# A gated recurrence over 512 steps on one core: input gates placed in PSUM a pair of steps ahead, 512-column projections, and operands that arrive laid out

## The reference, cut to what matters

```python
Xz, Xr, Xh = (einsum('btc,hc->tbh', X, Wx) + bx for each gate)   # all steps at once
def step(H, xs):                                                  # 512 times, one after the other
    Z = sigmoid(xz + H @ Whz.T + bhz)
    R = sigmoid(xr + H @ Whr.T + bhr)
    H_tilda = tanh(xh + R * H @ Whh.T + bhh)
    H_new = Z * H + (1.0 - Z) * H_tilda
    Y = H_new @ Whq.T + bhq
out = x + transpose(Ys)
```

## Time and profile before

| | us |
|---|---|
| median of 3 runs (2405.9 to 2407.41) | 2407.05 |
| the profiled execution's own time | 2406.99 |
| its span, first to last instruction | 2405.2 |
| TensorE busy | 2346.3 (98%) |
| VectorE busy | 1732.1 (72%) |
| ScalarE busy | 1036.9 (43%) |

### The profile page before, as it was taken

One profiled execution on the slowest core, in us unless ns is written; L12 is line 12 of the kernel. 1 busy time (PEld: TensorE's weight loads), 2 busy tenths in 40 slices (PEclk: granted clock), 3 DMA queues, 4 the chain that ended last, 5 costly groups with the idle time before them and its releaser, 6 DMA issues.

```text
span 2405.2 us, 125877 instructions
## 1 busy us (share of the span) xinstructions
PE 2346.3 (98%) x54656; PEld 1969.8 (82%) x54656; DVE 1732.1 (72%) x10587; ACT 1036.9 (43%) x5144; POOL 0.8 (0%) x7
## 2 busy tenths in 40 slices
PE   7999999999999999999999999999999999999997
PEld 6888888888888888888888888888888888888875
DVE  5777777777777777777777777777777777777776
ACT  4444444444444444444444444444444444444443
POOL 0000000000000000000000000000000000000000
PEclk9999999999999999999999999999999999999999
DMA  5010110110100101101101001010011010110000
GB/s 163 12 30 21 30 30 12 30 29 21 30 16 25 30 21 30 28 14 29 29 21 30 16 25 30 21 30 25 16 30 27 23 30 14 28 30 21 21 14 18
DMA packets 60685, 66.06 MB, mean 27 GB/s; under 512 B 7201, under 2 KB 40033, under 8 KB 60129
## 3 DMA queue, kind: packets, MB, share of 16 engines
q1 hardware_dynamic: 60128, 58.00, 8.8%
HBM read 41.20 MB, written 16.78 MB: 24 GB/s over the span
## 4 chain that ended last, share of the span: by engine, by line
PE 80%; DVE 18%; issue 2%; DMA 0%; SPq 0%; ACT 0%; DVEq 0%
PE pre L335 45%; PE x_bank L306 26%; DVE pre_t L525 10%; PE y_bank L318 8%; DVE pre L532 6%; DVE reset_state L539 2%; DVE w_split L476 0%; DMA x_in<-in_x 0%; PE pre L289 0%; SPq L210 0%; PE y_bank L289 0%; DVE x_turned L489 0%; DVE fresh L546 0%; DVE kept L590 0%; DVE state L554 0%
## 5 line engine op out<-in xcount | busy, mean ns | idle before, releaser
L335 PE MATMUL pre<-w_gate,state 128*16 128x128 f32 x32768 | 995.5, 273 | 17.1 <-DVE state L554 16.5
L335 PEld LDWEIGHTS pre<-w_gate,state 128*16 128x16 f32 x32768 | 849.0, 97 | 120.2 <-DVE state L554 66.6
L525 DVE STREAM_TRANSPOSE pre_t<-pre 128x32 f32<-128x32 f32 (+1 forms) x3072 | 456.1, 200 | 623.0 <-PE pre L335 618.4
L306 PE MATMUL x_bank<-x_part,w_split 128*128 128x256 f32 x4608 | 645.4, 289 | 0.8 <-DVE w_split L476 0.8
L306 PEld LDWEIGHTS x_bank<-x_part,w_split 128*128 128x128 f32 x4608 | 568.9, 188 | 79.5 <-issue 79.5
L335 PE MATMUL pre<-w_gate,reset_state 128*16 128x128 f32 x16384 | 546.3, 274 | 25.2
L335 PEld LDWEIGHTS pre<-w_gate,reset_state 128*16 128x16 f32 x16384 | 402.2, 96 | 169.2 <-DVE reset_state L539 169.2
L532 DVE STREAM_TRANSPOSE pre<-x_gate 128x128 f32<-128x128 f32 x1024 | 399.0, 390 | 1.0 <-PE pre L374 1.0
L437 ACT ACTIVATE r_gate<-pre_t 128x16 f32<-128x16 f32 (+1 forms) x1536 | 234.5, 215 | 354.2 <-DVE pre_t L525 354.2
L450 ACT COPY states<-state 128x64 f32<-128x64 f32 x512 | 160.5, 313 | 403.7 <-DVE state L554 403.7
L439 ACT ACTIVATE z_gate<-z_pre 128x64 f32<-128x64 f32 x512 | 131.6, 257 | 419.7 <-DVE z_pre L585 419.7
(11 more groups left out here) (38 smaller groups left out, 394.8 us busy)
## 6 DMA issues: line engine op xcount, KB each, us to landing
x_in<-in_x SPq DMA_DIRECT2D x256, 64.0 KB, 2.4
y_out<-in_x SPq DMA_DIRECT2D x64, 256.0 KB, 3.6
out<-y_out SPq DMA_DIRECT2D x64, 256.0 KB, 2.8
w_raw<-in_L_cond_Wxr SPq DMA_DIRECT2D x1, 1024.0 KB, 6.0
w_raw<-in_L_cond_Wxz SPq DMA_DIRECT2D x1, 1024.0 KB, 7.0
w_raw<-in_L_cond_Wxh SPq DMA_DIRECT2D x1, 1024.0 KB, 9.4
w_raw<-in_L_cond_Whr SPq DMA_DIRECT2D x1, 1024.0 KB, 7.9
w_raw<-in_L_cond_Whz SPq DMA_DIRECT2D x1, 1024.0 KB, 8.3
```

The source lines that it names most:

```text
L306: mm = nc.tensor.matmul(x_bank[k % 2][:, 0:ROWS], w_split[w][:, g, m, P * m_out:P * (m_out + 1)], x_part[a][:, m, :], start=(u == 0), stop ...
L335: mm = nc.tensor.matmul(pre[g][Q * j:Q * j + B, 0:P], of[:, m, :], w_gate[g][:, m, P * j:P * (j + 1)], start=(g == Z and m == 0), stop=(m ...
L525: nc.vector.transpose(pre_t[g][:, a:b].rearrange("p m b -> p (m b)"), pre[g][:, Q * a:Q * b]).then_inc(pre_turned[g][h], 1)
```

## The change

- Two banks for R and H together and two for Z, used by **pairs of steps** in turn. The even step's result goes to the rows 0 to 15 of each strip and the odd step's to 16 to 31. For that the odd step's stationary operand is **32 columns wide**: 16 columns of zeros and then the 16 of the state. The even step's stays at 16.
- `put_x` writes x's part of both steps of a pair at once, for **all three gates**, one pair ahead: R and Z at the start of an even step, H at the start of an odd one, before the turning of R. The add for Z (`z_pre`) is gone.
- x is projected in tiles of 32 steps, 512 columns a matmul (the first and last tile have 16 steps). Six matmuls, half a group, stand behind H in six of eight steps, and half a block of the outputs in the other two. In the first tile a whole group (12 matmuls of 512 columns) stands behind H of the steps 2 to 13. ScalarE copies a finished group of 512 columns in the next step.
- The high part of each new state is made step by step by ScalarE (128x64) and its low part by **GpSimd**, which also makes the low parts of x (pieces of 128x256, one in each of the steps 12 to 15 of every 16) and adds the output's bias (128x512, one in 8 steps).
- x, the weights, the first state and the biases come in the layout in which the kernel uses them, and the output goes back by blocks of 8 steps, so that the turning of weights and of x on TensorE and VectorE is gone. The rearrangement is made outside the timed execution.

The core of the diff. Where x's projection stands:

```diff
+    def x_work(t):
+        n = tile_of(t)
+        start, size = tiles[n]
+        s = t - start
...
+        if n == 0:
+            return [(1, s - 2, 0, U)] if 2 <= s < 2 + GATES else []
+        if s % YS in Y_PLACES:
+            return []
+        u = ((s // YS) * len(X_PLACES) + s % YS) * (U // 2)
+        return [(n + 1, u // U, u % U, u % U + U // 2)]
```

TensorE's `recur`:

```diff
             def recur(g, t):
+                par, s = t // 2 % 2, t % 2
+                if s == 0:
+                    pe.wait_ge(x_put[g], t // 2 + 1)
...
-                    of = reset_state if g == H else state
+                    if g == H:
+                        of = reset_state[:, m, B:2 * B] if s == 0 else reset_state[:, m, :]
+                    else:
+                        of = states[:, 1 - par, m, 2 * B:3 * B] if s == 0 else states[:, par, m, 0:2 * B]
+                    rows = B if s == 0 else 2 * B
                     for j in range(G):
-                        mm = nc.tensor.matmul(pre[g][Q * j:Q * j + B, 0:P], of[:, m, :],
-                                              w_gate[g][:, m, P * j:P * (j + 1)],
-                                              start=(g == Z and m == 0), stop=(m == G - 1),
+                        mm = nc.tensor.matmul(gate_bank(g, par)[Q * j:Q * j + rows], of,
+                                              wh[g][:, m, P * j:P * (j + 1)], start=False, stop=(m == G - 1),
```

VectorE, one step:

```diff
-                        turn_pre(R, t, h)
-                    put_x(H, par, step)
-                    for h in range(N):
-                        reset(t, h)
...
+                if k + 1 < pairs:
+                    for g in ((R, Z) if s == 0 else (H,)):
+                        put_x(g, k + 1)
+                dve.wait_ge(pre_done[R], t + 1)
+                for h in range(N):
+                    turn(R, t, PARTS[h], r_turned[h])
+                for h, (a, b) in enumerate(PARTS):
+                    dve.wait_ge(r_ready[h], t + 1)
+                    nc.vector.tensor_tensor(reset_state[:, a:b, B:2 * B], r_gate[:, a:b], old[:, a:b], ALU.mult
...
+                if t % YS < 2 and t >= 2 * YS:
+                    add_y(t // YS - 2, t % YS)
...
+                if t >= 4:
+                    dve.wait_ge(s_lo_ready, t - 3)
```

GpSimd, one step:

```diff
+                for d, c in split_work(t):
+                    take_x_lo(d, c)
+                if t % YS == 0 and t >= YS:
+                    add_bias(t // YS - 1)
+                pool.wait_ge(s_hi_ready, t + 1)
+                nc.gpsimd.tensor_tensor(s_part[LO][:, t // YS % 2, :, s_cols(t)], state_after(t),
+                                        s_part[HI][:, t // YS % 2, :, s_cols(t)].bitcast(F32), ALU.subtract
```

ScalarE, one step:

```diff
+                if t:
+                    for d, k in x_done(t - 1):
+                        copy_x_gate(d, k)
+                for d, c in split_work(t):
+                    take_x_hi(d, c)
...
+                nc.scalar.copy(s_part[HI][:, t // YS % 2, :, s_cols(t)], state_after(t)).then_inc(s_hi_ready, 1)
```

More of the change, by code:

```diff
@@ L184, in gru @@
-        SPLIT_MATS = [0, 1, 2, last_mat]
-        def split_place(mat, a, m):
-            return w_split[a][:, mat if mat < 3 else 3, m, :]
-        def flat(t):
[L191 to L202, removed]
+        def flat(t):
+            return t.rearrange("p m b -> p (m b)")
@@ new lines, in x_piece, with raw_piece, split_work @@
+        def x_piece(d, c):
+            half, m = divmod(c, G)
+            cols = tiles[d][1] * B // 2
+            return m, slice(half * cols, (half + 1) * cols)
+        def raw_piece(d, c):
+            m, cols = x_piece(d, c)
+            if d < 2:
+                return (x_raw if d == 0 else x_gate[:, 1, Z])[:, m, cols]
+            return x_raw[:, m, 0:cols.stop - cols.start]
+        def split_work(t):
+            n = tile_of(t)
+            start, size = tiles[n]
+            s = t - start
+            pieces = [(1, s * G + c) for c in range(G)] if n == 0 and s < 2 else []
+            if n + 2 <= last_tile and s % (size // 2) >= size // 2 - G:
+                pieces.append((n + 2, s // (size // 2) * G + s % (size // 2) - (size // 2 - G)))
+            return pieces
@@ L205, in _ @@
         @block.sync
         def _(sp):
[L207 to L247, removed]
@@ L261, in _, with load_x, load_half_x @@
[L261 to L266, removed]
+            def load_x(to, start, count, done):
+                sp.dma_start(to[:, :, 0:count * B], x_t[:, :, start * B:(start + count) * B]).then_inc(done, 16)
+            def load_half_x(d, half):
+                start, size = tiles[d]
+                sp.wait_ge(x_lo_ready, d * PIECES + half * G if (d, half) != (2, 0) else PIECES)
+                load_x(x_raw, start + half * size // 2, size // 2, x_loaded)
@@ new lines, in _ @@
+            for u in range(2):
+                load_residual(u)
+            for u in range(blocks):
+                n = tile_of(u * YS)
+                place = u - tiles[n][0] // YS
+                if n + 2 <= last_tile and place * YS in (0, tiles[n][1] // 2):
+                    load_half_x(n + 2, place > 0)
+                if u >= 2:
+                    store(u - 2)
+                    sp.wait_ge(stored[u % 2], (u // 2) * 16)
+                    load_residual(u)
+            for u in (blocks - 2, blocks - 1):
+                store(u)
@@ new lines, in project_y @@
+            def project_y(u, first, end):
+                if first == 0:
+                    pe.wait_ge(s_lo_ready, (u + 1) * YS)
+                    if u >= 2:
+                        pe.wait_ge(y_added, 2 * (u - 1))
+                for k in range(first, end):
+                    a, w, m = UNITS[k]
+                    mm = nc.tensor.matmul(y_bank[u % 2][:], s_part[a][:, u % 2, m, :], w_part[3][w][:, m, :],
+                                          start=(k == 0), stop=(k == U - 1))
+                if end == U:
@@ L376, in _ @@
-            mm.then_inc(banks_primed, 1)
-            tile_loop(pe, tile)
-            project_states(2 * tiles - 1, 1, 0, len(UNITS))
+            pe.wait_ge(zeroed, 2)
+            for par in range(2):
+                for g in range(3):
+                    for j in range(G):
+                        mm = nc.tensor.matmul(gate_bank(g, par)[Q * j:Q * (j + 1)], reset_state[:, 0, :],
+                                              flat(reset_state[:]), start=(g != H), stop=True,
+                                              skip_group_check=(g == H))
@@ new lines, in _ @@
+            mm.then_inc(banks_primed, 1)
+            pe.wait_ge(x_lo_ready, PIECES)
+            for g in range(3):
+                pe.wait_ge(w_lo_ready, (g + 1) * G)
+                for m_out in range(G):
+                    project_x(0, g * G + m_out, 0, U)
+            for t in range(steps):
+                recur(R, t)
+                recur(Z, t)
+                recur(H, t)
+                for d, k, first, end in x_work(t):
+                    if k == 0 and first == 0:
+                        pe.wait_ge(x_lo_ready, (d + 1) * PIECES)
+                    project_x(d, k, first, end)
+                for u, first, end in y_work(t):
+                    if u == 0 and first == 0:
+                        pe.wait_ge(w_lo_ready, 4 * G)
+                    project_y(u, first, end)
@@ L452, in _, with take_w_hi @@
-            for half in range(2):
-                copy_x_hi(0, half, is_first=True)
-            for what, k in SETUP:
-                if what == "turn":
-                    copy_mat(k)
-                else:
-                    act.wait_ge(bias_ready, 1)
-                    for m_out in range(G):
-                        copy_x_gate(0, k * G + m_out, 0)
-            tile_loop(act, tile)
-            copy_states_hi(2 * tiles - 1, 1, False)
+            def take_w_hi(g, m):
+                if m == 0:
+                    act.wait_ge(wx_loaded[g], 16)
+                nc.scalar.copy(w_part[g][HI][:, m], w_raw(g)[:, m]).then_inc(w_hi_ready, 1)
```

613 lines of the change are left out of this document (262 added, 351 removed).

## The result

The changed kernel takes **2370.35 us** (median of 4 runs, 2369.54 to 2370.88) against 2406.85 for the kernel before in the same session (2405.9 to 2407.41), a ratio of 0.985 with a 95% interval of 0.983 to 0.986. That is faster, as forecast, and inside the range of 2315 to 2404, but 20 us above the forecast of 2350. The profiled execution took 2370.61 with a span of 2368.8, 36.4 less than the span before.

A forecast was written before the change was run, and what follows sets the result against it. Bound: the R-to-H chain plus TensorE's work from H to R. From 2407, -74 (full tiles) + 15 - 3 (first, last tile) - 14 + 1 - 1 (setup, end) + 7 (loads) + 12 (GpSimd) = -57: 2350 us, range 2315 to 2404.

The forecast's parts named there:

- What bounds the kernel: Each step is the chain from R to H (1.99) plus TensorE's work from H to R (2.6); TensorE idles 0.23 us.
- the floor of 1.76: Earliest start of H after R by TensorE's own work; forecast as not reached, rival reaching it 2307 us, chance 0.06.
- R to H: From R's start to H's: moving H's write ahead of R's result gives 1.85 instead of 1.99, 0.14 us less a step.
- H to R, 2.59: From H's start to the next R's, with six 512-column matmuls behind H in full tiles: 2.59, saving 0.02.
- First tile, +15: In 12 steps of the first tile, twelve 512-column matmuls behind H make 5.85 instead of 4.60: +15 us.
- Wider weights, +7: Loads of 32 columns in odd steps cost 13 ns more, waited for only at the first of R and H: +7 us.
- the rival beside that rule: Rival: weight loads are not hidden at all, every odd-step set 13 ns longer: 80 us, 2423 us, chance 0.03.
- GpSimd, +12: GpSimd's SBUF work meets VectorE's `reset` in four steps of 16: between 0 and 24 us, half taken, +12.
- the slower rival: Rival: GpSimd's two-operand work takes twice as long and `reset` waits for its end: 129 instead of 12, 2467 us, chance 0.08.
- Ahead of the loop, -14: Setup before the recurrence: R first starts at 31 to 33 instead of 46, -14 us.
- the forecast's own range: Range of the main forecast: 2318 (no GpSimd cost, 0.02 less on the chain, setup 5 shorter) to 2385 us.

The follow-up runs named there:

- e4_before_put_moved: The kernel before, with VectorE's write of x's part for H moved ahead of the turning of R: 2347.82 us, ratio 0.976 to the kernel before.
- e1_h_wait_off: The changed kernel without TensorE's wait for `x_put` of H ahead of H's matmuls in even steps: 2347.73 us.
- e2_split_first: The changed kernel with ScalarE's casts of x and Whq put ahead of its copy of the finished gate group: 2358.09 us.
- e6_all_wide: The changed kernel with 32-column stationary operands in even steps too, the second half an old state, so not computing the reference: 2377.38 us.
- e7_single_steps: e3_both without pairs: 16 columns in every step and three writes of x's part a step, one step ahead: 2327.76 us.
- e8_gpsimd_busy: e3_both with a further GpSimd subtraction of 128x1024 in every step: 2923.21 us (one run).
- e3_both: The changed kernel with the edits of e1_h_wait_off and e2_split_first, and no TensorE wait for `x_put` after the first pair: 2334.10 us.

## Why the prediction was right, and where it was off

- **What bounds the kernel** was read rightly: a 98% busy TensorE with a stop of 0.23 in each step, of which the write ahead of `reset` held 0.13. e4_before_put_moved moves nothing else and wins 58 us, 2.4%. The other 0.10, from 1.864 down to the floor of 1.76, no run here removed.
- **R to H, "1243.77, or 1.85 after R".** Measured 1.864 with loads of 16 columns. The failing step is that `reset` "takes 0.15": 0.15 was its length while it queued behind the write. When it waits for ScalarE itself it takes 0.18, and H follows its start by 0.23, not 0.21. That is 0.014 x 480 = 7 us. Its start was put well, 1.64 after R against 1.63 measured.
- **The added wait for `x_put` was left out of the sum.** The prediction does not mention it: its sum from `reset` to H has `reset`'s length and the 0.06 behind it, and nothing for a further wait. It costs 0.091 in the even steps, 22.6 us in all (e1_h_wait_off). This is the largest term that the forecast missed. The wait is not free if it stands on the queue between the last event of the chain and the instruction that it releases.
- **H to R, 2.59**: 2.60. Not counted was that the last tile has only 16 steps and so halves the columns behind H in the tile before it: 2.34 there, 8 us less.
- **First tile, +15**: +21. The splitting of Whq on ScalarE and VectorE in the steps 4 to 7 stood ahead of R's turning and cost 1.1 us in each; e2_split_first, which changes that order, brings the first tile back to +16.
- **Wider weights, +7**: e6_all_wide measures 7 for the even steps and e7_single_steps 6 for the odd ones. So the 13 ns was priced right, but it is not the first load that is waited for (e6_all_wide). The Trainium skill (TensorE: Matmul & The Clock Gate, "The mechanism") says that loads overlap with running matmuls only where the row group differs. This case's traces do not agree for column strips that all use the same rows: 7 us came, where the rival beside that rule had put 80. The same section also lets a load run ahead into a background weight buffer; no run here shows whether that is the reason.
- **GpSimd, +12**: 60 x 0.105 = 6. The durations were put well (0.6 and 1.2; measured 0.73 and 1.28), and so was the time of the late pieces (end 1.9 after R; measured 1.89, with `reset` starting at 1.63). What was mis-sized is the price of the wait. The sum took 0.3 for a held `reset` and half a chance of it; the wait is real, but `reset` ends 0.03 after GpSimd's instruction, and that is 0.11 later than it would have ended. The bias ends at 1.66, 0.03 into `reset`, and lengthens it by nothing. The mechanism of the slower rival is real, as e8_gpsimd_busy shows. The Trainium skill (SBUF — State Buffer, "Who interferes with whom") says that the two contend and calls the ports that they share an exclusive lock, and both traces agree.
- **Ahead of the loop, -14**: -14.2.
- **The range.** The lower end of the forecast's own range, 2318, does not follow from the three terms named with it: 2350 - 12 - 10 - 5 = 2323. Errors of both signs met: without the 8 us of the shorter tile and the 6 us that GpSimd did not cost, the kernel would have taken some 2384, still inside the stated range.

The sum over the full tiles: 19 for wide loads and GpSimd were forecast above 1.85 and 2.59. What came between R and H is 1.930 - 1.85 = 0.080 a step or 38, of which the added wait is 22 (240 x 0.091), `reset`'s length 7 (480 x 0.014), GpSimd 6 and the wide loads 3 (240 x 0.014). H to R is 5 more than put (448 x 0.011), and the shorter tile gives 8 back. That makes 35 in place of 19. The kernel before took 1 more in this stretch than the sum had put, and so the table shows a difference of 15.

## What to carry to other kernels

On a latency chain through several engines, look at each in-order queue for work that stands between the last event and the next instruction, and move it to where that engine waits anyway: one moved line was worth 2.4% here, more than the rewrite around it. Count a new wait as an instruction if it shares its place with the wait that really ends the chain, even when its own event is long past; drop it where program order on the other engine already gives it. Where the engine's own work ends last, as ahead of R in the full tiles, the same wait cost nothing. Before work goes to GpSimd, place it in time against VectorE's two-operand instructions of the critical chain, since these do not finish until it is done.

## What the runs showed of the hardware

- A second semaphore wait on a TensorE instruction appears as an instruction of 51 ns ahead of it. It cost 0.09 us behind the event that ends the chain (e1_h_wait_off), 0.07 to 0.08 ahead of R in the last 48 steps, and nothing where TensorE's own work ended last (e3_both). In the profile the idle time ahead of H is called "issue".
- On GpSimd a subtraction takes 0.32 us for 128x64, 0.73 for 128x256 and 2.36 for 128x1024, and an addition 1.28 for 128x512. A two-operand VectorE instruction in SBUF that starts meanwhile ends no sooner than 0.03 after it (the changed kernel, e8_gpsimd_busy); a turning from PSUM is not held up.
- A weight load of 32 columns has a mean of 110 ns against 97 for 16. In a row of matmuls the difference is hidden; behind the first set of a gate that has been waited for it costs about 0.013 us (e6_all_wide).
